# The last items of an attention stage and the start of the MLP: another order of masks, exponentials, one product and the low parts

## The chip, the cores and the metric

One core of a Trainium2 chip runs the whole program. TensorE (PE) does all products, VectorE (DVE), ScalarE (ACT) and GpSimd (POOL) the elementwise work, and SyncE (SP) issues every DMA. The metric is the device time of one execution in microseconds.

## What is computed

The input is 16 items of 128 tokens by 512 channels. Three stages follow each other: A is self attention with a mask, B is attention over a context, D is a gated attention at the end, and between B and D stands an MLP (512 to 2048 to 512). The part of the reference that matters here is the end of B and the MLP:

```
scores = jnp.einsum('bhqd,bhkd->bhqk', q, k) / jnp.sqrt(jnp.float32(HD))
scores = scores * mask - 10000.0 * (1.0 - mask)
probs = jax.nn.softmax(scores, axis=-1)
ctx = merge_heads(jnp.einsum('bhqk,bhkd->bhqd', probs, v))
x = x + ctx @ w_co + b_co
ln_out = layernorm(x, ln3_s, ln3_b)
mlp_out = gelu(ln_out @ w1 + b1) @ w2 + b2
```

There are 16 heads of 32 channels. Each fp32 operand of a large product is kept as a high part (rounded copy) and a low part (the rest), and a product is the sum of high by high, high by low and low by high.

## The kernel before

The program for each engine is written out by hand, engine by engine, and every wait is on a semaphore. An engine works strictly through its own list. Items are numbered g = 0 to 47 (16 to 31 are stage B). For an item PE makes `scores(g)`, DVE scales and masks them (`mask_scores`, two halves), POOL adds the mask bias (`add_mask_bias`, two halves), DVE takes the row maxima (`row_max`), ACT the exponentials in four quarters (`exps(g, 0..3)`), and DVE inverts the row sums (`inverse_sums`, L1825). PE then turns the inverted sums (`row_sums(g)`, L954) and the probabilities (`transpose_prob`, L933) through PSUM. ACT and DVE copy the turned probabilities back (`prob_out`, ACT quarters 0 and 2, DVE quarters 1 and 3), PE multiplies by the values (`times_v(g)`, L991), and after a split of the context into parts, `project_out(g)` (L1014). The turned row sums go out by ACT (`row_sums_out`, L1418) and over two DMAs of SP (`store_row_sums`, `spread_row_sums`) into the tile that `context(g)` reads.

The function `last_steps_of_b`, one per engine, handles items 30 and 31. In it PE has the MLP's first products between the attention's: `w1(p)` (L1075) makes 256 hidden channels of the first 256 tokens, and `w2(p)` (L1094) brings them back to 512. ACT adds the bias and squares (`hidden_out(p)`, L1496 and L1501), DVE makes the argument of the tanh (L1906), ACT the tanh (L1481), and DVE the high (`gelu_hi`, L1889 and L1897) and the low part (`gelu_lo`, L1901) that `w2(p)` waits for. `hidden_out(p)` also empties the PSUM bank: `project_out(28)` writes the bank of `w1(1)`, and `project_out(29)` that of `w1(3)`, so these two wait for the bias step of `hidden_out(1)` and `hidden_out(3)` (the semaphore `s_hx`).

Weights come in units of four chunks. `split((unit, c))` on ACT (L1337) makes a chunk's high part, on POOL (L2228) its low part. Units 12 and 14 are the third and fourth quarter of w1, 13 and 15 of w2. SP loads 13 and then 12 in step 13 of stage B, and 14 only after it has stored and spread the row sums of item 31:

```
store_row_sums(31)
spread_row_sums(31)
load_stream(31)
for c in range(KC):
    load_chunk((14, c))
```

`mlp_fill(1)` are the inputs for the second group of tokens, needed from `w1(8)` on: `turn_inputs` and `fill_hi` on DVE, `fill_scale` on ACT, `fill_lo` on POOL. PE's order from item 31 on is `times_v(29)`, `scores(31)`, `w1(2)`, `row_sums(30)`, transposes, `w1(3)`, transposes, `project_out(29)`, `times_v(30)`, `w1(4)`, `row_sums(31)`, transposes, `w2(0)`, `project_out(30)`, transposes, first half of `w2(1)`, `times_v(31)`, second half of `w2(1)`, `project_out(31)`, `w2(2)`, `w1(5)`, `w2(3)`, `w1(6)`, and on in this alternation.

Of the kernel before, what the change touches and what calls it, by code (L numbers as in the profile page):

```python
# [8 lines left out]
KC = H // 128  # L9
# [126 lines left out]
CHUNKS += [(u, c) for u in (12, 13, 14, 15, 16, 17, 18, 19) for c in range(KC)]  # L136
# [137 lines left out]
def build(nc, x, first_x, enc, encT, mask_a, mask_b, mask_d, weights, columns, rows, gate, ident_in, out):  # L274
# [3 lines left out]
    with ExitStack() as ctx:  # L278
# [566 lines left out]
        def pe_program():  # L845
# [232 lines left out]
            def w2(p, tiles=None):  # L1078
# [5 lines left out]
                if group.first == 0 and j % 2 == 0:  # L1084
                    pe.wait_ge(s_wlo, max(LO_COUNT[W2_UNIT[n], c] for c in range(KC)))
# [88 lines left out]
            def last_steps_of_b():  # L1174
# [18 lines left out]
                w1(4)  # L1193
                row_sums(31)
                transpose_prob(31, 0)
                transpose_prob(31, 1)
                w2(0)
# [133 lines left out]
        def act_program():  # L1331
# [230 lines left out]
            def last_steps_of_b():  # L1562
                for b in (14, 15):
                    g = 16 + b
                    if b == 14:
                        context_hi(g - 2, 0)
                        context_hi(g - 2, 1)
                    else:
                        tanh(0)
                    row_sums_out(g - 1)  # L1570
                    hidden_out(2 * b - 28)
                    prob_out(g - 1, 0)
                    for c in range(2 * b - 28, 2 * b - 26):
                        split((12, c))
                    hidden_out(2 * b - 27)
                    prob_out(g - 1, 2)
                    exps(g, 0)
                    exps(g, 1)
                    exps(g, 2)
                    if b == 14:  # L1580
                        context_hi(29, 0)
                        context_hi(29, 1)
                    exps(g, 3)
# [6 lines left out]
                for c in range(KC):  # L1590
                    split((13, c))
# [86 lines left out]
            for c in range(KC):  # L1678
                split((14, c))
            for p in range(5, NG * NPAIR):  # L1680
                g, jp = divmod(p, NPAIR)
                tanh(p - 1)
                hidden_out(p)
                if (g, jp) == (0, 5):
                    for c in range(KC):
                        split((15, c))
                    fill_scale(mlp_fill(1))
# [23 lines left out]
        def dve_program():  # L1711
# [300 lines left out]
            def last_steps_of_b():  # L2012
                for b in (14, 15):
                    g = 16 + b
                    context(g - 2, 0)
                    context(g - 2, 1)
                    if b == 14:
                        inverse_sums(g - 1)
                    context_lo(g - 2, 0)
                    context_lo(g - 2, 1)  # L2020
                    if b == 15:
# [412 lines left out]
```

## Time and profile before

| | us |
|---|---|
| median of 3 runs | 1086.4 |
| lowest and highest | 1083.62, 1086.55 |
| the profiled execution: its time | 1087.28 |
| the profiled execution: its span | 1085.7 |
| PE busy | 1066.5 (98%) |
| DVE, ACT, POOL busy | 820.6, 704.0, 483.4 |

The span is the time between the first and the last instruction of the profiled execution, and the time is 1.58 us more. The granted clock of TensorE is 1.00 in every stretch, its upper level. The last two items of B with the first MLP products stand between 466 and 545 us of the span.

### The profile page before, as it was taken

To read this page: it belongs to the slowest core of one execution; us is meant where nothing else is said; L and a number is where in the kernel's file an instruction comes from. 1 tells how busy PE (TensorE), PEld (TensorE's weight loads), DVE (VectorE), ACT (ScalarE), POOL (GpSimd) and SP (SyncE) were. 2 spreads that over 40 slices of the span, in tenths; PEclk is the share of its full clock that TensorE was granted. 3 is DMA by queue.
4 is the path that set the end of the run, shared out by engine and by line. 5 is a ranking of instruction groups with operands and counts; after the bars stand their busy time and mean duration, and the time that the engine had idled before them with its cause. 6 is when DMAs were issued, how large, how long until landed. Compare 5 with 4: busy or idle time off the path is not lost.

```text
span 1085.7 us, 24226 instructions
## 1 busy us (share of the span) xinstructions
PE 1066.5 (98%) x8741; PEld 924.1 (85%) x8741; DVE 820.6 (76%) x1303; ACT 704.0 (65%) x2355; POOL 483.4 (45%) x361
## 2 busy tenths in 40 slices
PE   8999999999999999999999999999999999999998
PEld 7889888888888888887898888888888998888886
DVE  8788777777888787888867667767697467777667
ACT  5787778677778787786444444444455276666676
POOL 4776555566777776767513122113032233333210
PEclk9999999999999999999999999999999999999999
DMA  7366666577777777564252151341647647777621
GB/s 248 104 190 209 202 206 192 187 190 223 221 217 216 222 216 227 180 193 139 85 155 98 59 174 59 117 141 53 214 136 257 229 127 207 223 209 210 195 61 60
DMA packets 145927, 185.92 MB, mean 171 GB/s; under 512 B 17952, under 2 KB 88848, under 8 KB 145808
## 3 DMA queue, kind: packets, MB, share of 16 engines
q1 hardware_dynamic: 145808, 184.37, 54.9%
q8 instruction: 70, 1.15, 0.5%
q14 instruction: 49, 0.40, 0.1%
HBM read 122.59 MB, written 61.73 MB: 170 GB/s over the span
## 4 chain that ended last, share of the span: by engine, by line
PE 66%; DVE 11%; DMA 7%; ACT 6%; POOL 4%; SPq 4%; issue 3%; DVEq 0%; ACTq 0%; POOLq 0%
PE psum L895 17%; PE psum L1094 15%; PE psum L1075 14%; PE psum L887 7%; PE psum L1014 6%; POOL prob L2267 3%; PE psum L913 2%; ACT prob L1409 2%; PE psum L991 2%; DMA ln_tile<-stream 2%; DMA normalised<-ln_tile 2%; DVE ln_tile L1739 2%; PE psum L933 2%; DVE negmax L1817 1%; SPq L558 1%
## 5 line engine op out<-in xcount | busy, mean ns | idle before, releaser
L895 PE MATMUL psum<-inputs_hi,weights_hi 128*128 128x256 f32 x768 | 224.2, 292 | 2.0 <-POOL inputs_lo L2253 1.4
L895 PE MATMUL psum<-inputs_lo,weights_hi 128*128 128x256 f32 x768 | 217.1, 283 | 0.0
L895 PE MATMUL psum<-inputs_hi,weights_lo 128*128 128x256 f32 x768 | 216.9, 282 | 0.0
L2267 POOL TENSOR_TENSOR prob<-prob,mask_bias 128x1024 f32<-128x1024 f32 x64 | 153.1, 2413 | 93.8 <-DVE prob L1804 93.2
L895 PEld LDWEIGHTS psum<-inputs_hi,weights_hi 128*128 128x128 f32 x768 | 146.6, 191 | 8.5 <-issue 2.9
L1817 DVE TENSOR_REDUCE negmax<-prob 128x8 f32<-128x1024 f32 x96 | 115.8, 1212 | 49.3 <-POOL prob L2267 49.1
L1409 ACT ACTIVATE prob<-prob,negmax 128x128 f32<-128x128 f32 x384 | 148.3, 391 | 0.5 <-DVE negmax L1817 0.5
L895 PEld LDWEIGHTS psum<-inputs_lo,weights_hi 128*128 128x128 f32 x768 | 147.0, 191 | 0.2
L895 PEld LDWEIGHTS psum<-inputs_hi,weights_lo 128*128 128x128 f32 x768 | 146.9, 191 | 0.0
L2253 POOL TENSOR_TENSOR inputs_lo<-inputs_transposed,inputs_hi 128x512 fp32r<-128x512 f32 x70 | 93.5, 1357 | 94.3 <-DVE inputs_hi L1777 60.5
L1409 ACT ACTIVATE prob_blocks<-prob,negmax 128x128 f32<-128x128 f32 x304 | 117.8, 391 | 19.4 <-DVE negmax L1817 19.3
L1014 PE MATMUL psum<-weights_hi,context_parts 128*128 128x512 f32 x376 | 125.8, 394 | 0.6 <-ACT qT L1355 0.3
L1496 ACT ACTIVATE qT<-psum,columns 128x512 f32<-128x512 f32 (+1 forms) x80 | 46.2, 598 | 96.9 <-PE psum L1075 96.9
L2270 POOL TENSOR_TENSOR residual<-residual,bias_rows 128x512 f32<-128x512 f32 x42 | 59.7, 1425 | 77.9 <-DMA residual<-stream 58.8
L1094 PE MATMUL psum<-weights_hi,hidden_parts 128*128 128x512 f32 x264 | 87.6, 392 | 1.1 <-DVE hidden_parts L1901 1.0
L1906 DVE SCALAR_TENSOR_TENSOR kT<-kT,qT 128x512 f32<-128x512 f32 x64 | 47.2, 737 | 51.9 <-ACT kT L1501 51.7
L1014 PEld LDWEIGHTS psum<-weights_hi,context_parts 128*128 128x128 f32 x376 | 70.7, 188 | 16.6 <-ACT qT L1496 0.6
L2228 POOL TENSOR_TENSOR weights_lo<-weights_whole,weights_hi 128x512 fp32r<-128x512 f32 x56 | 75.1, 1356 | 20.4 <-ACT weights_hi L1337 20.4
L1094 PE MATMUL psum<-weights_hi,context_parts 128*128 128x512 f32 x248 | 81.7, 390 | 0.9 <-DVE context_parts L1901 0.9
L1804 DVE SCALAR_TENSOR_TENSOR prob<-psum,mask 128x512 f32<-128x512 f32 x128 | 79.2, 680 | 2.9 <-ACT gate L1671 2.9
L1447 ACT ACTIVATE inputs_transposed<-inputs_transposed,columns 128x256 f32<-128x256 f32 x120 | 62.3, 590 | 27.6 <-DVE inputs_transposed L1746 27.6
L1075 PE MATMUL psum<-hidden_inputs,weights_hi 128*128 128x512 f32 x256 | 78.8, 389 | 0.0
(138 smaller groups left out, 2657.0 us busy)
## 6 DMA issues: line engine op xcount, KB each, us to landing
weights_whole<-weights_in SPq DMA_DIRECT2D x80, 256.0 KB, 3.8
prob_turned<-prob_blocks SPq DMA_DIRECT2D x38, 512.0 KB, 3.0
prob<-prob_turned SPq DMA_DIRECT2D x152, 128.0 KB, 3.5
inputs_transposed<-normalised SPq DMA_DIRECT2D x120, 128.0 KB, 2.8
normalised<-ln_tile SPq DMA_DIRECT2D x24, 512.0 KB, 2.8
context<-row_sums_spread SPq DMA_DIRECT2D x188, 64.0 KB, 2.1
stream<-residual SPq DMA_DIRECT2D x42, 256.0 KB, 2.9
ln_tile<-stream SPq DMA_DIRECT2D x32, 256.0 KB, 4.1
```

The source lines that it names most:

```text
L887: mm = pe.matmul(ps[:, bank, :], a[:, buf, c, tok], w[:, slot, c, :], start=c == 0 and i == 0, stop=c == KC - 1 and i == 2)
L895: mm = pe.matmul(ps[:, bank, GT * part:GT * part + GT], w[:, slot, c, o], a[:, buf, c, :], start=c == 0 and i == 0, stop=c == KC - 1 and i ...
L1014: mm = pe.matmul(ps[:, U_BANK + 1, :], a[0][:, cs], w[:, slot, c, :], start=c == 0 and i == 0, stop=c == KC - 1 and i == 2)
L1075: mm = pe.matmul(out, w[:, slot, c, o], a, start=c == 0 and i == 0, stop=c == KC - 1 and i == 2)
L1094: mm = pe.matmul(ps[:, accumulator(group, t), :], a[gb][:, tok], w[:, slot, (j * chunks + e) % 4, :], start=j == 0 and e == 0 and i == 0, ...
L1409: ins = act.activation(dst, src, ACT.Exp, bias=negmax[:, par, s:s + 1], accum_out=total[:, par, s:s + 1])
L1447: ins = act.activation(dst, src, ACT.Identity, bias=cols[:, b0 + c:b0 + c + 1], scale=cols[:, g0 + c:g0 + c + 1])
L1804: ins = dve.scalar_tensor_tensor(heads(P[:, 512 * c:512 * c + 512]), ps[:, S_BANK:S_BANK + 4, T * c:T * c + T], SCALE, other.unsqueeze(1). ...
L1817: dve.tensor_reduce(negmax[:, par, 8 * h:8 * h + 8], heads(prob[:, par, 1024 * h:1024 * h + 1024]), AX.X, ALU.max, negate=True).then_inc(s ...
L2228: pool.tensor_tensor(wlo[:, slot, c, :], raw[:, slot, c, :], whi[:, slot, c, :].bitcast(f32), ALU.subtract).then_inc(s_wlo, 1)
L2253: pool.tensor_tensor(lo, y, hi.bitcast(f32), ALU.subtract).then_inc(s_rlo if fill.ln is None else s_flo, 1)
L2267: pool.tensor_tensor(half, half, mb.unsqueeze(1).to_broadcast([128, 8, T]), ALU.add).then_inc(s_biased, 1)
```

## The change

It reorders work at the end of stage B and at the start of the MLP, on four engines; SP's list is untouched, and no engine has an operation more or less.

- DVE: the masking of items 30 and 31 goes ahead of the low parts of the context, and `inverse_sums` stands between or behind the halves. `prob_out` and `row_max` change places for item 31, and `prob_out(30, 3)` goes between `gelu_hi(0)` and `gelu_lo(0)`. `fill_hi(mlp_fill(1))` moves from step 5 to step 6, behind `gelu_lo(5)`.
- ACT: `exps(30, 0)` goes ahead of `hidden_out(1)`, `exps(31, 0)` ahead of `hidden_out(3)`, and `tanh(0)` behind `hidden_out(2)`. The splits of units 13 and 14 change places. `fill_scale(mlp_fill(1))` goes to step 6, ahead of `hidden_out(6)`, and the splits of unit 15 behind it.
- PE: `w2(0)` goes ahead of `row_sums(31)`, and `w2` of the first group waits chunk by chunk for the low parts of its weights.
- POOL: the splits of unit 14 wait for `s_glo` 3, that is for `gelu_lo(2)`; then come those of 13; `fill_lo(mlp_fill(1))` goes ahead of the splits of 15.

```diff
-CHUNKS += [(u, c) for u in (12, 13, 14, 15, 16, 17, 18, 19) for c in range(KC)]
+CHUNKS += [(u, c) for u in (12, 14, 13, 15, 16, 17, 18, 19) for c in range(KC)]
...
-                if group.first == 0 and j % 2 == 0:
-                    pe.wait_ge(s_wlo, max(LO_COUNT[W2_UNIT[n], c] for c in range(KC)))
+                if group.first == 0:
+                    pe.wait_ge(s_wlo, LO_COUNT[W2_UNIT[n], (j * chunks + chunks - 1) % 4])
...
                 w1(4)
+                w2(0)
                 row_sums(31)
                 transpose_prob(31, 0)
                 transpose_prob(31, 1)
-                w2(0)
...
+                context_hi(28, 0)
+                context_hi(28, 1)
+                row_sums_out(29)
+                hidden_out(0)
+                prob_out(29, 0)
+                split((12, 0))
+                split((12, 1))
+                exps(30, 0)
+                hidden_out(1)
+                prob_out(29, 2)
+                exps(30, 1)
+                exps(30, 2)
+                context_hi(29, 0)
+                context_hi(29, 1)
+                exps(30, 3)
+                row_sums_out(30)
+                hidden_out(2)
+                prob_out(30, 0)
+                tanh(0)
+                split((12, 2))
+                split((12, 3))
+                exps(31, 0)
+                hidden_out(3)
+                prob_out(30, 2)
+                exps(31, 1)
+                exps(31, 2)
+                exps(31, 3)
                 context_hi(30, 0)
                 context_hi(30, 1)
                 tanh(1)
...
                 prob_out(31, 0)
                 tanh(2)
                 for c in range(KC):
-                    split((13, c))
+                    split((14, c))
                 prob_out(31, 2)
                 hidden_out(4)
                 context_hi(31, 0)
...
             tanh(3)
             for c in range(KC):
-                split((14, c))
+                split((13, c))
             for p in range(5, NG * NPAIR):
                 g, jp = divmod(p, NPAIR)
                 tanh(p - 1)
+                if (g, jp) == (0, 6):
+                    fill_scale(mlp_fill(1))
                 hidden_out(p)
-                if (g, jp) == (0, 5):
+                if (g, jp) == (0, 6):
                     for c in range(KC):
                         split((15, c))
-                    fill_scale(mlp_fill(1))
...
+                context(28, 0)
+                context(28, 1)
+                make_mask_bias(30)
+                mask_scores(30, 0)
+                inverse_sums(29)
+                mask_scores(30, 1)
+                context_lo(28, 0)
+                context_lo(28, 1)
+                prob_out(29, 1)
+                row_max(30, 0)
+                row_max(30, 1)
+                prob_out(29, 3)
+                normalise(mlp_fill(1))
+                tanh_argument(0)
+                stream(28)
+                context(29, 0)
+                context(29, 1)
+                make_mask_bias(31)
+                mask_scores(31, 0)
+                mask_scores(31, 1)
+                inverse_sums(30)
+                context_lo(29, 0)
+                context_lo(29, 1)
+                row_max(31, 0)
+                prob_out(30, 1)
+                row_max(31, 1)
+                gelu_hi(0)
+                prob_out(30, 3)
+                gelu_lo(0)
+                tanh_argument(1)
+                stream(29)
...
+                    if g == 0:
+                        fill_hi(mlp_fill(1))
                     tanh_argument(p)
...
                 attention_residual(30)
+                attention_residual(31)
+                pool.wait_ge(s_glo, 3)
                 for c in range(KC):
-                    split((13, c))
-                attention_residual(31)
+                    split((14, c))
```

On ACT, at the start of step 30 before the change, from the last copy of item 29's quarter 0 on (`waits` are the semaphores; `w_hi` and `hidden` tell of weights and of `w1`):

```order
L1387 ACTIVATE prob<-psum 128x512 [waits prob_transposed]
L1337 ACTIVATE weights_hi<-weights_whole 128x512 [waits chunk0_loaded]
L1337 ACTIVATE weights_hi<-weights_whole 128x512 [waits chunk1_loaded]
L1496 ACTIVATE qT<-psum,columns 128x256 [waits hidden]
L1496 ACTIVATE qT<-psum,columns 128x256
L1501 ACTIVATE kT<-qT 128x512 [waits hidden_plus_bias]
L1387 ACTIVATE prob<-psum 128x512 [waits prob_transposed]
```

The same place after the change:

```order
L1387 ACTIVATE prob<-psum 128x512 [waits prob_transposed]
L1337 ACTIVATE weights_hi<-weights_whole 128x512 [waits chunk0_loaded]
L1337 ACTIVATE weights_hi<-weights_whole 128x512 [waits chunk1_loaded]
L1409 ACTIVATE prob,total<-prob,negmax 128x128 [waits row_sum_inverse,row_max]
L1409 ACTIVATE prob,total<-prob,negmax 128x128 x3
L1496 ACTIVATE qT<-psum,columns 128x256 [waits hidden]
L1496 ACTIVATE qT<-psum,columns 128x256
L1501 ACTIVATE kT<-qT 128x512 [waits hidden_plus_bias]
L1387 ACTIVATE prob<-psum 128x512 [waits prob_transposed]
```

Four exponentials now stand between the splits and the bias step of `hidden_out(1)`; item 31 has the same pattern with `hidden_out(3)`.

On PE, behind `w1(4)`, before the change (L954 is `row_sums(31)`, L1094 is `w2(0)`, whose first tile is shown):

```order
L1075 MATMUL psum<-inputs_hi,weights_lo 128x256
L954 MATMUL psum<-identity,rtotal 16x128 [waits stream_updated,row_sum_inverse]
L933 MATMUL psum<-identity,prob 128x128 [waits ctx_normalised,exps]
L933 MATMUL psum<-identity,prob 128x128 x3
L933 MATMUL psum<-identity,prob 128x128 [waits ctx_normalised,exps]
L933 MATMUL psum<-identity,prob 128x128 x3
L1094 MATMUL psum<-weights_hi,hidden_parts 128x512 [waits masked,w_lo,gelu_lo]
```

The same place after the change, with the whole of `w2(0)`:

```order
L1075 MATMUL psum<-inputs_hi,weights_lo 128x256
L1094 MATMUL psum<-weights_hi,hidden_parts 128x512 [waits masked,w_lo,gelu_lo]
L1094 MATMUL psum<-weights_lo,hidden_parts 128x512
L1094 MATMUL psum<-weights_hi,hidden_parts 128x512 x2
L1094 MATMUL psum<-weights_lo,hidden_parts 128x512
L1094 MATMUL psum<-weights_hi,hidden_parts 128x512
L1094 MATMUL psum<-weights_hi,hidden_parts 128x512 [waits masked]
L1094 MATMUL psum<-weights_lo,hidden_parts 128x512
L1094 MATMUL psum<-weights_hi,hidden_parts 128x512 x2
L1094 MATMUL psum<-weights_lo,hidden_parts 128x512
L1094 MATMUL psum<-weights_hi,hidden_parts 128x512
L954 MATMUL psum<-identity,rtotal 16x128 [waits stream_updated,row_sum_inverse]
```

The row sums of item 31, and all that follows from them on ACT and SP, now stand behind twelve products.

## Rows read from the trace of the kernel before

**Rows 1.** A stretch of the MLP: us, busy time of each engine (x instructions), clock, DMA

```profile
700.00:750.00 50.00, 50.00 (x222) 41.42 (x221) 36.28 (x55) 21.20 (x35) 15.18 (x12) 1.00 0.30 95
```

**Rows 2.** Timeline of PE: start us, length us, instruction [idle before it <-releaser]

```profile
476.00 0.50 PE L1014 MATMUL psum<-weights_hi,context_parts 128*128 128x512 f32 x1
...
481.07 0.39 PE L1075 MATMUL psum<-inputs_hi,weights_hi 128*128 128x256 f32 x1
...
485.16 0.28 PE L954 MATMUL psum<-identity,rtotal 128*16 128x128 f32 x1 [0.94 <-DVE rtotal L1825]
...
490.13 0.50 PE L1014 MATMUL psum<-weights_hi,context_parts 128*128 128x512 f32 x1
...
498.50 0.28 PE L954 MATMUL psum<-identity,rtotal 128*16 128x128 f32 x1 [1.19 <-DVE rtotal L1825]
...
499.42 0.47 PE L1094 MATMUL psum<-weights_hi,hidden_parts 128*128 128x512 f32 x1
...
502.27 0.39 PE L1014 MATMUL psum<-weights_hi,context_parts 128*128 128x512 f32 x1
...
507.33 1.08 PE L991 MATMUL psum<-prob,v 128*32 128x128 f32 x32
...
509.97 0.50 PE L1014 MATMUL psum<-weights_hi,context_parts 128*128 128x512 f32 x1
...
514.04 0.50 PE L1094 MATMUL psum<-weights_hi,hidden_parts 128*128 128x512 f32 x1 [1.03 <-DVE hidden_parts L1901]
...
532.13 0.50 PE L1094 MATMUL psum<-weights_hi,context_parts 128*128 128x512 f32 x1 [0.94 <-DVE context_parts L1901]
```

**Rows 3.** Timeline of ACT, end of B

```profile
475.11 0.84 ACT L1496 ACTIVATE qT<-psum,columns 128x256 f32<-128x256 f32 x2 [0.57 <-PE psum L1075]
...
483.18 0.39 ACT L1409 ACTIVATE prob<-prob,negmax 128x128 f32<-128x128 f32 x1
...
484.72 0.61 ACT L1481 ACTIVATE kT<-kT 128x512 f32<-128x512 f32 x1
...
489.24 0.84 ACT L1496 ACTIVATE qT<-psum,columns 128x256 f32<-128x256 f32 x2 [0.60 <-PE psum L1075]
...
499.16 0.25 ACT L1418 ACTIVATE row_sums_transposed<-psum 16x128 f32<-16x128 f32 x1
...
501.57 2.18 ACT L1337 ACTIVATE weights_hi<-weights_whole 128x512 fp32r<-128x512 f32 x4
505.63 0.60 ACT L1387 ACTIVATE prob<-psum 128x512 f32<-128x512 f32 x1 [1.89 <-PE psum L933]
```

**Rows 4.** Timeline of DVE, end of B and start of the MLP

```profile
469.51 0.26 DVE L1825 RECIPROCAL rtotal<-total 128x16 f32<-128x16 f32 x1 [1.07 <-ACT prob L1409]
...
470.63 2.48 DVE L1804 SCALAR_TENSOR_TENSOR prob<-psum,mask 128x512 f32<-128x512 f32 x4
...
474.44 1.22 DVE L1817 TENSOR_REDUCE negmax<-prob 128x8 f32<-128x1024 f32 x1 [0.73 <-POOL prob L2267]
...
510.89 1.41 DVE L1897 TENSOR_SCALAR hidden_parts<-kT 128x512 fp32r<-128x512 f32 x1
...
519.87 0.43 DVE L1897 TENSOR_SCALAR hidden_parts<-kT 128x512 fp32r<-128x512 f32 x1
...
526.13 2.10 DVE L1777 CAST inputs_hi<-inputs_transposed 128x512 fp32r<-128x512 f32 x2 [2.15 <-ACT inputs_transposed L1447]
```

**Rows 5.** Timeline of POOL: the two mask-bias halves of item 30

```profile
471.99 4.76 POOL L2267 TENSOR_TENSOR prob<-prob,mask_bias 128x1024 f32<-128x1024 f32 x2 [2.25 <-DVE prob L1804]
```

**Rows 6.** Timeline of SP's queue: the store of item 31's row sums

```profile
499.44 0.32 SPq L675 DMA_DIRECT2D row_sums_spread<-row_sums_transposed  x1
```

**Rows 7.** Tile weights_whole, 502.5 to 506 us: ns min/median/max, first and last start; landing

```profile
L617 SPq DMA_DIRECT2D weights_whole<-weights_in x4: 376/383/1105, 503.1 to 505.3; - x4
...
L2228 POOL TENSOR_TENSOR weights_lo<-weights_whole,weights_hi x3: 1292/1481/1738, 502.3 to 504.9; 128x512 fp32r<-128x512 f32 x3
...
DMA to landing us min/median/max: 3.6/3.8/4.2
```

More of the change, by code:

```diff
@@ L1562, in last_steps_of_b @@
             def last_steps_of_b():
[L1563 to L1583, printed above, removed]
+                context_hi(28, 0)
[25 more added lines that the diff above has]
+                exps(31, 3)
                 context_hi(30, 0)
@@ L2012, in last_steps_of_b @@
             def last_steps_of_b():
[L2013 to L2021, printed above, removed]
-                        inverse_sums(g - 1)
-                    make_mask_bias(g)
-                    mask_scores(g, 0)
-                    mask_scores(g, 1)
-                    prob_out(g - 1, 1)
-                    row_max(g, 0)
-                    row_max(g, 1)
-                    prob_out(g - 1, 3)
-                    if b == 14:
-                        normalise(mlp_fill(1))
-                    if b == 15:
-                        gelu_hi(0)
-                        gelu_lo(0)
-                    tanh_argument(b - 14)
-                    stream(g - 2)
+                context(28, 0)
[29 more added lines that the diff above has]
+                stream(29)
                 context(30, 0)
@@ L2193, in dve_program @@
                     turn_inputs(mlp_fill(1))
-                    fill_hi(mlp_fill(1))
                 if jp == (4 if g == 1 else 5) and 0 < g < NG - 1:
@@ L2350, in pool_program @@
             for c in range(KC):
-                split((14, c))
+                split((13, c))
             pool.wait_ge(s_row, 48)
@@ L2362, in pool_program @@
                     inverse_deviation(FILLS_OF_MLP[g][1])
-                if (g, jp) == (0, 5):
-                    for c in range(KC):
-                        split((15, c))
+                if (g, jp) == (0, 6):
                     fill_lo(mlp_fill(1))
+                    split((15, 0))
+                    split((15, 1))
                 if jp == 4 and ending:
@@ L2378, in pool_program @@
                     inverse_deviation(FILLS_OF_MLP[1][0])
+                    split((15, 2))
+                    split((15, 3))
             fill_lo(ln_fill(3, 1, 1))
```

## The prediction

> **What bounds the kernel now.** I read the busy shares first: TensorE is busy for 98% of the span, so nothing counts but what makes PE wait, or stop waiting. I then read the table of stretches: from 550 to 800 us PE has no idle time at all, as in [rows 1], where it is busy 50.00 of 50 us at the full clock. A delay or a gain that PE has at 540 us is therefore handed on unchanged to the end. So I went through the waits of PE and its timeline only between 466 and 545 us, where the change lies. PE idles there in four places [rows 2]: 0.94 us ahead of the row sums of item 30 and 1.19 us ahead of those of item 31 (both released by DVE's `inverse_sums`), 1.03 us ahead of `w2(2)` and 0.94 us ahead of `w2(5)` (both released by DVE's `gelu_lo`). They come to 4.1 us, which is the most that the change can take away, 0.38% of the time. Last I followed ACT, DVE, POOL and SP's queue through the same stretch, to see what each waiting instruction really hangs on.
>
> **Masks and exponentials of item 30.** Before, DVE idles 1.07 us for the last exponentials of item 29 (so from 468.44 on) and masks item 30 only from 470.63, in 2.48 us for both halves [rows 4]. The first half can now be done at about 468.44 + 0.2 + 1.24 = 469.9. POOL's bias takes 4.76 / 2 = 2.38 us a half [rows 5], so it ends at 472.3, and the row maximum of 1.22 us [rows 4], behind one copy, at about 474.1. ACT had been free since 475.11 - 0.57 = 474.54 and waited for `w1(1)` [rows 3]. It now starts `exps(30, 0)` there. A quarter takes 484.72 - 483.18 = 1.54 us [rows 3]. But `hidden_out(1)` stands behind it: it starts at 476.08 where it started at 475.11, its bias step ends 0.84 us later, and `project_out(28)`, which waits for that step to empty its bank, moves from 476.00 to 476.97. **A wait of 0.97 us is added here.** What PE would have found ahead of `row_sums(30)` is now used up: it ran out of work at 485.16 - 0.94 = 484.22 and now does so at 485.19. The inverse sums are there by then: scores(31) end when `w1(2)` starts, 481.07 before and about 482.1 now [rows 2], both masks take 2.48 us to 484.6, and the reciprocal 0.26 us to 484.85. So `row_sums(30)` stands at 485.2 as before at 485.16, and nothing is won by item 30.
>
> **Exponentials of item 31.** ACT was free at 489.24 - 0.60 = 488.64 ahead of `hidden_out(3)` [rows 3]. The tanh of the first product, now behind the row sums instead of ahead of them, moves this to about 489.1 (one instruction of 0.61 us, pipelined to 0.5). `exps(31, 0)` then ends at 490.6 and the bias step at 491.45. `project_out(29)` moves from 490.13 to about 491.5: **1.35 us are added**. From its start to the end of `w1(4)` PE has 498.50 - 1.19 - 490.13 = 7.18 us of work [rows 2], so it ends at 498.65. The 1.19 us wait would be gone by this alone.
>
> **`w2(0)` ahead of the row sums.** `w2(0)` takes 502.27 - 499.42 = 2.85 us [rows 2] and starts at about 498.5. So `row_sums(31)` goes from 498.50 to about 501.2, and `project_out(30)` stands at 502.1 where it stood at 502.27. Up to here PE has exchanged 0.94 + 1.19 us of one kind of wait for 0.97 + 1.35 us of another, and 0.15 us is won by the pipeline.
>
> **What hangs on these row sums.** This is the step that decides. ACT's `row_sums_out(31)` ended at 499.16 + 0.25 = 499.41; it began 0.66 us behind the transpose, when ACT had other work; now ACT waits for it, and I take 0.3, so that it ends at about 501.75. SP's store of the row sums followed at 499.44 [rows 6], then their spread, and the four loads of unit 14 from 503.1 on [rows 7]. All of this is in SP's fixed order and moves by 2.3 us. The last of the four was issued at 505.3, and they land 3.8 us after issue (3.6 to 4.2) [rows 7]: 509.1 before, 511.4 now. Before the change, ACT took unit 13 at this place, which had long been loaded: four splits from 501.57 in 2.18 us, and it then waited 1.89 us for the turned probabilities, so `prob_out(31, 2)` began at 505.63 [rows 3]. Now unit 14 stands there, ahead of `prob_out(31, 2)`. The last split ends at 511.4 + 0.6 = 512.0 and the copy of 0.60 us at 512.6. `times_v(31)` needs this copy, and behind it on PE stand half of `w2(1)` and `project_out(31)`; on ACT stand `hidden_out(4)` and `context_hi(31)`. **`times_v(31)` moves from 507.33 to 512.6, that is by 5.3 us.**
>
> From there to `project_out(31)` are 509.97 - 507.33 = 2.64 us, and twelve products take 2.85 us [rows 2]. `w2(2)` would so have come at 512.82 and came at 514.04. The wait ahead of it falls away: `gelu_lo(2)` ended 514.04 - 507.33 = 6.7 us behind the start of `times_v(31)`. Of this 1.0 us goes since POOL is held back (1.41 us of scaling at 510.89, 0.43 at 519.87 [rows 4]), and a tanh argument of 0.7 us is done during the wait. I take 5 us, so 517.6 (at worst 5.7, 0.2 us behind PE). `w2(2)` comes at 512.6 + 2.64 + 2.85 = 518.1: **4.1 us later than before**.
>
> **The fill and the low parts.** DVE waited 2.15 us for ACT's scaling ahead of `fill_hi(mlp_fill(1))` [rows 4], and `gelu_hi(5)` stood behind it; hence the wait ahead of `w2(5)`. Now `gelu_hi(5)` and `gelu_lo(5)` come first, and this wait goes: **1.1 us are won** (0.94 idle and 0.16 us in which the pipeline drains; both ends 0.9 and 1.2). POOL now waits for `gelu_lo(2)` at 517.6, and unit 14's four low parts take 1.29 to 1.74 us each [rows 7], median 1.48: done at 523.5. `w1(6)` wants them three products of 2.85 us behind `w2(2)`, at 526.6; unit 13's follow ahead of `w2(4)` and `w2(5)`, chunk by chunk. I cost this at nothing, and the cover is 3.1 us.
>
> **The sum.** 4.1 - 1.1 = +3.0 us; the roundings above lean late, so I take +2.9. On the profiled execution's 1087.28 us that is 1090.2; this one lies 0.9 us above the median of the runs, so against 1086.4 it is 1089.3. Bounds: one of SP's four issues took 1105 ns where the median is 383 [rows 7]; if that does not recur, 0.7 us less. Landing at 3.6 or 4.2 us moves it by -0.2 to +0.4. The two added waits can be off by 0.5 us together. The likeliest case's own range is 1087.8 to 1090.4.
>
> The four loads landed 3.8 us after issue [rows 7]. The Trainium skill, DMA: Bandwidth & Descriptors, Anatomy of one DMA, fits 2.0 us plus bytes over 436 GB/s for the path issued from GpSimd, which as an estimate gives 2.6 us for these 256 KB. By that page the last load would land 1.2 us sooner and the time would be 1088.1. The trace does not agree with it here, and the sum goes by the row.
>
> **The rivals.** First, **the loads do not hold ACT up**. Then `times_v(31)` comes at about 507.2, `w2(2)` at 512.7 (-1.3), and with the fill's 1.1 us the time is 1084.0. If the two waits for `hidden_out` don't arise either, up to 1.7 us more goes, to 1082.3. For it speaks that each step does shorten the chain it is aimed at, and that DVE scales in 0.43 us without POOL beside it and in 1.41 us with it [rows 4]. Against it speaks SP's order, which nothing changes: the last load would have to land before about 504.5, and 509.1 was its landing even with the earlier row sums. This decides the sign. Chance 14%, of which 8 points lie below 1083.1. The Trainium skill, SBUF — State Buffer, Who interferes with whom, says that GpSimd and such a VectorE instruction hold a common port in turn, for the whole instruction, and so backs the gain from holding the low parts back; the trace agrees with it in these two rows.
>
> Second, **the held-back low parts become a wait of their own**. If `gelu_lo(2)` comes later than 520.7 instead of 517.6, or POOL needs over 2.25 us a chunk, `w1(6)` waits, and on top of the 2.9 us come up to 2 more: 1091.3. The 3.1 us of cover speak against it, and the longest chunk of 1.74 us. Chance 12%, with any other added wait.
>
> Third, **the waits cancel**: with SP's short issue and quick landing the load wait costs 2 us less, and the result is 1087.3, no measurable change. Chance 14%. The forecast keeps 60%.
>
> **How the numbers follow.** A measurement of this kernel can tell about 0.3%, 3.3 us, from no change: above 1089.7 is slower, below 1083.1 faster. The forecast at 1089.3 lies just inside; its own range reaches 0.7 us beyond the bound, and 28 of its 60 points lie there. With the second rival's 12, slower has 0.40. Faster has 0.08, from the first rival. Within the bound are 32 + 6 + 14 points, 0.52. The range 1085.5 to 1091.2 leaves out most of the first rival and the worst of the second.
>
> **What the profile would show.** The first step is right if PE waits ahead of `project_out(28)` and `project_out(29)` for ACT's bias step, and L954 no longer waits. The deciding step is right if PE idles about 5 us ahead of `times_v(31)`, released by ACT, whose splits idle for a DMA. If ACT's splits run without idling, or PE's wait there is under 3 us, I am wrong. `w2(5)` should have no wait, and `w1(6)` none for POOL.

## The result, and the profile after

The changed kernel takes 1100.12 us (median of 4 runs, 1098.86 to 1102.46), beside 1086.47 us (4 runs, 1083.62 to 1086.87) for the kernel before on the same chip: a ratio of 1.0129 (95% interval 1.0115 to 1.0144). It is slower by 13.7 us where 2.9 us were forecast. The profiled execution has a span of 1099.4 us, 13.7 us more than before, and a mean granted clock of 0.994 instead of 1.00.

PE's timeline after the change, between 475 and 560 us (start, length, instruction, idle time before it and what ended it):

```profile
475.84 0.63 PE L933 MATMUL psum<-identity,prob 128*128 128x128 f32 x4 [0.64 <-DVE prob L1847]
479.27 0.80 PE L1014 MATMUL psum<-weights_hi,context_parts 128*128 128x512 f32 x1 [2.80 <-ACT qT L1496]
...
484.69 1.07 PE L991 MATMUL psum<-prob,v 128*32 128x128 f32 x24
...
507.03 0.27 PE L954 MATMUL psum<-identity,rtotal 128*16 128x128 f32 x1
...
507.93 0.48 PE L1014 MATMUL psum<-weights_hi,context_parts 128*128 128x512 f32 x1
...
519.42 1.94 PE L991 MATMUL psum<-prob,v 128*32 128x128 f32 x32 [6.25 <-ACT prob L1387]
...
523.43 0.39 PE L1014 MATMUL psum<-weights_hi,context_parts 128*128 128x512 f32 x1
...
526.16 0.39 PE L1094 MATMUL psum<-weights_hi,hidden_parts 128*128 128x512 f32 x1
...
538.37 0.50 PE L1094 MATMUL psum<-weights_hi,hidden_parts 128*128 128x512 f32 x1 [0.84 <-DVE hidden_parts L1908]
...
557.00 0.50 PE L1094 MATMUL psum<-weights_hi,context_parts 128*128 128x512 f32 x1 [1.34 <-DVE context_parts L1908]
```

Line numbers are 7 to 15 higher than before for DVE and POOL. Beside [rows 2]: the waits of 0.94 and 1.19 us ahead of L954, of 1.03 us ahead of `w2(2)` (526.16) and of 0.94 us ahead of `w2(5)` are gone, 4.1 us as forecast. In their place stand 0.64, 2.80, 1.18 (item 31's transposes, at 495.62), 1.08 (`project_out(29)`, at 497.33), 6.25, 0.84 and 1.34 us, 14.1 us together. That is +10.0 us. The rest is no wait. `project_out(28)` runs from 479.27 to 484.69, 5.42 us; the same twelve products took 478.96 - 476.00 = 2.96 us before. `times_v(31)` takes 521.29 - 519.42 = 1.87 us, where 1.02 us were enough in the second experiment below. The table of stretches shows why (busy time of PE, PE's loads, DVE, ACT and POOL, then the granted clock):

```profile
479.00:485.00 6.00, 5.73 (x20) 4.10 (x24) 1.26 (x3) 4.41 (x19) 0.00 (x0) 0.50 0.48 161
485.00:513.00 28.00, 25.73 (x244) 22.39 (x236) 21.08 (x32) 16.77 (x60) 10.04 (x6) 1.00 0.29 89
513.00:519.00 6.00, 0.17 (x1) 0.00 (x0) 0.72 (x2) 2.63 (x5) 1.26 (x1) 0.74 0.80 272
519.00:523.00 4.00, 3.58 (x37) 2.77 (x38) 1.84 (x5) 3.26 (x8) 0.00 (x0) 0.54 0.00 0
```

The granted clock is at its lower level, 1.2 GHz (0.50), behind the 2.80 us of idling, and falls again in the 6.25 us. The first costs 5.42 - 2.96 = 2.46 us, the second 1.87 - 1.02 = 0.85 us on `times_v(31)` and 2.14 - 1.62 = 0.52 us on the half of `w2(1)` behind it. Waits and clock come to 10.0 + 3.8 = 13.8 us.

**Why 2.80 us.** DVE between 469 and 478 us, after the change:

```profile
469.88 1.22 DVE L1811 SCALAR_TENSOR_TENSOR prob<-psum,mask 128x512 f32<-128x512 f32 x2
471.02 4.07 DVE L1859 TENSOR_TENSOR context_parts<-context,context_parts 128x256 fp32r<-128x256 f32 x2
475.02 0.68 DVE L1847 COPY prob<-psum 128x512 f32<-128x512 f32 x1
475.62 2.33 DVE L1824 TENSOR_REDUCE negmax<-prob 128x8 f32<-128x1024 f32 x2
```

POOL beside it:

```profile
469.87 4.94 POOL L2282 TENSOR_TENSOR prob<-prob,mask_bias 128x1024 f32<-128x1024 f32 x2 [0.39 <-DVE prob L1811]
```

and ACT's exponentials of item 30:

```profile
476.85 0.40 ACT L1409 ACTIVATE prob<-prob,negmax 128x128 f32<-128x128 f32 x1 [2.62 <-DVE negmax L1824]
...
478.41 0.81 ACT L1496 ACTIVATE qT<-psum,columns 128x256 f32<-128x256 f32 x2
```

The low parts of the context (L1859, two inputs in SBUF) now lie beside POOL's mask bias, which also reads SBUF. The pair takes 4.07 us; in the kernel before it stood at 469.81 us, ahead of POOL's start, and took 0.76 us. It ends when POOL's pair ends (475.0 and 474.8). So the first row maximum comes at 476.8 instead of the 474.1 that I worked out, and the four exponentials hold ACT's bias step, and PE, until 479.2.

**Why 6.25 us.** ACT between 514 and 520 us, after the change:

```profile
514.40 0.63 ACT L1337 ACTIVATE weights_hi<-weights_whole 128x512 fp32r<-128x512 f32 x1 [4.24 <-DMA weights_whole<-weights_in]
516.72 0.63 ACT L1337 ACTIVATE weights_hi<-weights_whole 128x512 fp32r<-128x512 f32 x1 [1.69 <-DMA weights_whole<-weights_in]
517.62 1.27 ACT L1337 ACTIVATE weights_hi<-weights_whole 128x512 fp32r<-128x512 f32 x2 [0.27 <-DMA weights_whole<-weights_in]
518.79 0.58 ACT L1387 ACTIVATE prob<-psum 128x512 f32<-128x512 f32 x1
```

and the tile's loads from 510 us on:

```profile
L617 SPq DMA_DIRECT2D weights_whole<-weights_in x4: 376/379/382, 511.5 to 512.9; - x4
...
DMA to landing us min/median/max: 2.9/5.0/5.4
```

ACT waits 6.2 us for unit 14 ahead of the copy that `times_v(31)` needs. The issues were short this time (382 ns at most), but the landings took up to 5.4 us, 4.2 at most in [rows 7].

### The profile page after: what moved, and what is told of

Its sections match the earlier page's. It is cut to its first block, busy times and chain, and to the rows that moved or that the text cites. A ratio compares the mean times of both kernels' runs of the same rounds, so it can differ in the third digit from the quotient of the medians.

```text
span 1099.4 us, 24232 instructions
## 1 busy us (share of the span) xinstructions
PE 1070.3 (97%) x8741; PEld 926.9 (84%) x8741; DVE 826.2 (75%) x1303; ACT 704.0 (64%) x2355; POOL 482.9 (44%) x361
## 4 chain that ended last, share of the span: by engine, by line
PE 68%; DVE 12%; ACT 6%; DMA 5%; issue 3%; SPq 3%; POOL 2%; DVEq 0%; ACTq 0%
PE psum L895 18%; PE psum L1094 14%; PE psum L1075 14%; PE psum L887 7%; PE psum L1014 7%; PE psum L913 3%; PE psum L991 3%; POOL prob L2282 2%; DMA ln_tile<-stream 2%; DMA normalised<-ln_tile 2%; ACT prob L1409 2%; PE psum L933 2%; DVE ln_tile L1746 2%; DVE negmax L1824 1%; DVE context_parts L1859 1%
## 5 line engine op out<-in xcount | busy, mean ns | idle before, releaser
L1094 PE MATMUL psum<-weights_hi,hidden_parts 128*128 128x512 f32 x264 | 88.0, 394 | 0.9 <-DVE hidden_parts L1908 0.8
L1094 PE MATMUL psum<-weights_hi,context_parts 128*128 128x512 f32 x248 | 81.6, 390 | 1.3 <-DVE context_parts L1908 1.3
```

The costliest lines, as they stand in the source:

```text
L1094: mm = pe.matmul(ps[:, accumulator(group, t), :], a[gb][:, tok], w[:, slot, (j * chunks + e) % 4, :], start=j == 0 and e == 0 and i == 0, ...
```

## The experiments

The kernel before measured 1086.46 us (9 runs) beside the first four kernels below, 1087.41 us (29 runs) beside the next four and 1086.33 us (24 runs) beside the last four; every ratio is to its own set. The whole change was not run again in them: what is said against it is a difference of medians to its 1100.12 us, and the kernel before's own medians differ by 1.1 us. The first theory had three causes: DVE's low parts beside POOL, ACT's order, and the clock. Four kernels each undo or cover one of them in the whole change.

**DVE's low parts behind the row maxima**, the whole change otherwise (item 31 alike):

```diff
-                context_lo(28, 0)
-                context_lo(28, 1)
                 prob_out(29, 1)
                 row_max(30, 0)
                 row_max(30, 1)
+                context_lo(28, 0)
+                context_lo(28, 1)
```

> The changed kernel with VectorE's low parts of the context of items 28 and 29 moved from ahead of the row maxima of items 30 and 31 to behind them. Theory P (these two-operand subtractions stand still while GpSimd adds the mask bias; 4.07 and 4.04 us for two instead of 0.76): the pair takes under 1 us again, the row maximum of item 30 is ready near 474.1 instead of 476.8, project_out(28) waits about 1 us instead of 2.80 and the clock does not fall there; item 31 likewise. Time 6 to 8 us below the changed kernel, near 1093. Rival Q (the pair is slow wherever it stands, and the exponentials ahead of hidden_out cost the wait): no more than 1 us below it.

Measured: 1095.45 us (4 runs), ratio 1.0079 (1.0053 to 1.0106), 4.7 us less than the whole change. The first line of `project_out(28)` in PE's timeline:

```profile
473.30 0.50 PE L1014 MATMUL psum<-weights_hi,context_parts 128*128 128x512 f32 x1 [0.91 <-ACT qT L1496]
```

It waits 0.91 us, where 0.97 was forecast, and `times_v(29)` follows at 476.25, 2.95 us later: full clock. So the 2.80 us were the forecast's wait plus DVE's pair beside POOL. The gain is smaller than the 6 to 8 us expected: the pair still takes 1.83 us where it stands now, and the wait ahead of `times_v(31)` is 7.14 us instead of 6.25, with a landing of up to 6.2 us.

**ACT's copy ahead of the splits of unit 14**, the whole change otherwise:

```diff
                 tanh(2)
+                prob_out(31, 2)
+                hidden_out(4)
+                context_hi(31, 0)
+                context_hi(31, 1)
                 for c in range(KC):
                     split((14, c))
-                prob_out(31, 2)
-                hidden_out(4)
-                context_hi(31, 0)
-                context_hi(31, 1)
```

> The changed kernel with ScalarE's prob_out(31, 2), hidden_out(4) and context_hi(31) ahead of the four splits of unit 14. Theory L (the splits wait for loads that stand in SyncE's list behind the row sums, and TensorE waits for the copy behind them): the wait of 6.25 us ahead of times_v(31) goes, and so does the half clock behind it; 7 to 8 us below the changed kernel, near 1092.5. Rival M (the wait only moves: the high parts of unit 14 come too late for w1(6)): a wait ahead of w1(6) of several us, and 3 us or less below it.

Measured: 1093.36 us (5 runs), ratio 1.0059 (1.0038 to 1.0079), 6.8 us less than the whole change. `times_v(31)` has no wait and full speed:

```profile
511.60 1.08 PE L991 MATMUL psum<-prob,v 128*32 128x128 f32 x32
```

**Exponentials behind the bias step**, the whole change otherwise (item 31 alike):

```diff
-                exps(30, 0)
                 hidden_out(1)
                 prob_out(29, 2)
+                exps(30, 0)
```

> The changed kernel with exps(30, 0) and exps(31, 0) back behind hidden_out(1) and hidden_out(3) and their copies. Theory E (what stands ahead of hidden_out holds project_out up): no wait ahead of project_out(28), whose products run at full clock; the row sums of items 30 and 31 wait 1 to 3 us again, since the maxima stay late behind the blocked low parts; 3 to 5 us below the changed kernel. Rival (the exponentials cost nothing there, the late maxima alone do): the wait comes back in full at the row sums, and the time is within 1 us of the changed kernel.

Measured: 1094.41 us (5 runs), ratio 1.0063 (1.0043 to 1.0083), 5.7 us less. The waits ahead of `project_out(28)` and `project_out(29)` are gone, and none stands ahead of the row sums, where 1 to 3 us were expected: these places on ACT won nothing. DVE's late pair costs 0.50 and 1.16 us ahead of the transposes all the same. The gain lies above the 3 to 5 us expected.

**PE kept busy in the two gaps**, the whole change otherwise. Transposes of the identity matrix into a free bank, whose results nobody reads, are added:

```diff
+                    if b == 14:
+                        pe.wait_ge(s_masked, 62)
+                        keep_busy(24)
                     pe.wait_ge(s_hx, 2 * b - 26)
                     project_out(g - 2)
...
                 w2(1, (0,))
+                keep_busy(54)
                 times_v(31)
...
+                for k in range(times):
+                    pe.transpose(ps[:, S_BANK, 128 * (k % 4):128 * (k % 4) + 128], ident[:, :], ident[:, :])
```

> The changed kernel with 24 transposes of the identity ahead of TensorE's wait for hidden_out(1) and 54 ahead of times_v(31), into a PSUM bank that nobody reads then, so that it does not stand idle. Theory C (TensorE's clock falls to its lower level after the idle stretches of 2.80 and 6.25 us and the next products run at half speed): granted clock 1.00 throughout, twelve products of project_out(28) in 2.9 us instead of 5.4, times_v(31) in 1.0 instead of 1.9; 3 to 4 us below the changed kernel. Rival (the slow products are late operands): no gain, or up to 0.5 us lost to the transposes.

Measured: 1096.22 us (4 runs), ratio 1.0087 (1.0067 to 1.0107), 3.9 us less with every dependence as in the whole change, and one more for the free bank. `project_out(28)` takes 2.94 us and `times_v(31)` 1.01 us. But the clock then fell behind the next gaps. In PE's timeline:

```profile
490.77 0.63 PE L933 MATMUL psum<-identity,prob 128*128 128x128 f32 x4 [1.18 <-DVE prob L1856]
492.49 0.50 PE L1014 MATMUL psum<-weights_hi,context_parts 128*128 128x512 f32 x1 [1.09 <-ACT qT L1505]
...
497.02 1.08 PE L991 MATMUL psum<-prob,v 128*32 128x128 f32 x32
```

`project_out(29)` takes 497.02 - 492.49 = 4.53 us. The clock is a cost of its own, beside the idling.

**All three edits together, and then without the hold-back.** The first kernel is the whole change with the edits of the first three experiments. The second also drops one line of POOL:

```diff
-                pool.wait_ge(s_glo, 3)
```

> The changed kernel with all three edits of the first experiments at once: low parts of the context behind the row maxima, exps(30, 0) and exps(31, 0) behind hidden_out(1) and (3), ScalarE's copy ahead of the splits of unit 14. If ports, order ahead of hidden_out and the late loads are the whole loss: no wait over 0.5 us before w2(2), clock 1.00, and the time lies 1 to 3 us below the kernel before. If GpSimd's held-back low parts cost something by themselves (waits of 0.8 to 1.4 us ahead of w2(4) and w2(7) seen after the change): these two waits stay, and it is within 2 us of the kernel before.

> The same without GpSimd's wait for gelu_lo(2). Theory H (held back, the eight low parts of units 14 and 13 run in one piece beside VectorE's GELU steps, and each scaling takes 1.4 instead of 0.43 us): the wait ahead of w2(4) goes, w2(7) may keep its wait, a wait near 1 us ahead of w2(2) can come back; 0 to 1.5 us below the one with the hold. Rival (the waits come from the fill's new place): both stay.

Measured: 1087.16 us (12 runs), ratio 1.0002 (0.9989 to 1.0014), and 1086.71 us (12 runs), ratio 0.9997 (0.9984 to 1.0010). The three edits take back all but 0.2 us: they hold the whole loss. What stays of the change has no worth to be measured, with the hold-back or without. Its waits are others than before, not fewer, and the expectation of none over 0.5 us ahead of `w2(2)` failed: with the hold-back PE waits 0.58 us ahead of `project_out(28)`, 0.71 us ahead of `row_sums(30)` and 1.17 us ahead of `times_v(30)`, where the view names no releaser ("issue"); DVE's copy `prob_out(30, 3)`, one that it needs, ends at 492.84 us.

```profile
492.94 1.08 PE L991 MATMUL psum<-prob,v 128*32 128x128 f32 x32 [1.17 <-issue]
```

PE's waits behind 500 us, with the hold-back:

```profile
523.72 0.50 PE L1094 MATMUL psum<-weights_hi,hidden_parts 128*128 128x512 f32 x1 [1.26 <-DVE hidden_parts L1908]
...
542.37 0.50 PE L1094 MATMUL psum<-weights_hi,context_parts 128*128 128x512 f32 x1 [1.39 <-DVE context_parts L1908]
```

and without it:

```profile
510.38 0.50 PE L1014 MATMUL psum<-weights_hi,context_parts 128*128 128x512 f32 x1 [0.50 <-DVE context_parts L1859]
...
515.53 0.50 PE L1094 MATMUL psum<-weights_hi,hidden_parts 128*128 128x512 f32 x1 [2.06 <-DVE hidden_parts L1908]
```

The hold-back mainly chooses which steps of DVE lie beside POOL's eight low parts. With it these run in one row of 12.22 us, and the steps for `w2(4)` and `w2(7)` are late; without it, those for `project_out(31)` and `w2(2)`.

**The swap of units 13 and 14 alone**, in the kernel before:

```diff
-CHUNKS += [(u, c) for u in (12, 13, 14, 15, 16, 17, 18, 19) for c in range(KC)]
+CHUNKS += [(u, c) for u in (12, 14, 13, 15, 16, 17, 18, 19) for c in range(KC)]
...
                 tanh(2)
                 for c in range(KC):
-                    split((13, c))
+                    split((14, c))
                 prob_out(31, 2)
...
```

The later splits of ACT and both groups of POOL change places in the same way.

> The kernel before with only units 13 and 14 exchanged (ScalarE splits 14 ahead of prob_out(31, 2)), nothing else moved. Theory L: with the row sums at their old time the last load lands near 509, the copy ends near 510.3, TensorE waits about 3 us ahead of times_v(31), and 1.8 to 3.5 us are lost, more if the clock falls. Rival (the wait came from the later row sums alone): under 1 us lost.

Measured: 1092.9 us (4 runs), ratio 1.0051 (1.0031 to 1.0071). ACT waits 5.19 and 0.49 us for the loads, and PE waits twice for the change, ahead of `times_v(31)` and of `w2(2)`:

```profile
499.20 0.28 PE L954 MATMUL psum<-identity,rtotal 128*16 128x128 f32 x1 [2.31 <-DVE rtotal L1825]
...
511.09 1.08 PE L991 MATMUL psum<-prob,v 128*32 128x128 f32 x32 [3.00 <-ACT prob L1387]
512.10 0.63 PE L1094 MATMUL psum<-weights_hi,hidden_parts 128*128 128x512 f32 x1
...
514.66 0.63 PE L1014 MATMUL psum<-weights_hi,context_parts 128*128 128x512 f32 x1
...
520.05 0.50 PE L1094 MATMUL psum<-weights_hi,hidden_parts 128*128 128x512 f32 x1 [1.97 <-DVE hidden_parts L1901]
```

This edit alone costs 5.5 us, without `w2(0)` ahead of the row sums. It is more than the 1.8 to 3.5 us expected for a full clock, and the clock fell here in a place of its own: behind the gap of 3.00 us `times_v(31)` still took its full-clock time (1.01 us), and only the products after it were slow, the half of `w2(1)` with 514.66 - 512.10 = 2.56 us instead of 1.62. The 2.31 us ahead of the row sums stand ahead of anything that this edit touches (see the last section).

**The masks alone**, in the kernel before:

```diff
-                    if b == 14:
-                        inverse_sums(g - 1)
-                    context_lo(g - 2, 0)
-                    context_lo(g - 2, 1)
-                    if b == 15:
-                        inverse_sums(g - 1)
                     make_mask_bias(g)
                     mask_scores(g, 0)
+                    inverse_sums(g - 1)
                     mask_scores(g, 1)
+                    context_lo(g - 2, 0)
+                    context_lo(g - 2, 1)
```

> The kernel before with only VectorE's masking of items 30 and 31 ahead of the low parts of the context. Theory P: the two low parts take 4 us beside GpSimd's mask bias instead of 0.76, the copies of the turned probabilities behind them make TensorE wait 0.5 and 1.2 us, and the row sums still wait; 0.5 to 3 us slower than before. Rival (earlier masks help where nothing else is moved): 1 to 2 us faster.

Measured: 1084.36 us (10 runs), ratio 0.9976 (0.9963 to 0.9989). **I was wrong here**: I expected a loss from DVE's pair, and it is a gain. The pair does take 4.08 us beside POOL, but ACT now has `hidden_out(1)` ahead of the exponentials and waits for nothing. Only the transposes wait for DVE, and the row sums' waits shrink by more:

```profile
475.02 0.63 PE L933 MATMUL psum<-identity,prob 128*128 128x128 f32 x4 [0.52 <-DVE prob L1840]
...
495.98 0.28 PE L954 MATMUL psum<-identity,rtotal 128*16 128x128 f32 x1 [0.53 <-DVE rtotal L1825]
```

The late pair is harmless by itself, and dear with the exponentials ahead of the bias step: the 2.80 us need both. (For item 31 the order is not quite that of the change: `inverse_sums` stands between the halves, and the pair takes 2.97 us.)

**The fill alone**, in the kernel before (ACT, DVE and POOL as in the change, PE untouched; ACT's part is shown):

```diff
                 tanh(p - 1)
+                if (g, jp) == (0, 6):
+                    fill_scale(mlp_fill(1))
                 hidden_out(p)
-                if (g, jp) == (0, 5):
+                if (g, jp) == (0, 6):
                     for c in range(KC):
                         split((15, c))
-                    fill_scale(mlp_fill(1))
```

> The kernel before with one part of the change alone: the second fill (scaling on ACT, high part on DVE behind gelu_lo(5), low part on POOL ahead of unit 15) moved to step 6. Theory (the fill's own wait was a true stall and nothing stands behind it): the 0.94 us ahead of w2(5) go and no new wait takes their place, so about 1.0 us less than the kernel before, 1085.4 us, ratio 0.999. Rival (the time is only handed on): the high part now stands between two steps of the MLP on DVE and w2(6) or w2(7) waits 0.5 to 1.4 us, as w2(7) does after the whole change (1.34 us); then 1086.5 us, or up to 0.4 us more.

Measured: 1086.37 us (11 runs), ratio 0.9991 (0.9980 to 1.0003). The wait of 0.94 us ahead of `w2(5)` is gone, and one of 0.21 us, for POOL, stands ahead of `w2(6)`:

```profile
536.43 0.47 PE L1094 MATMUL psum<-weights_hi,hidden_parts 128*128 128x512 f32 x1 [0.21 <-POOL weights_lo L2230]
```

Between these two 0.7 us are won in the trace, but a gain that small isn't told from none by the times.

**`w2(0)` ahead of the row sums alone**, in the kernel before:

```diff
                 w1(4)
+                w2(0)
                 row_sums(31)
                 transpose_prob(31, 0)
                 transpose_prob(31, 1)
-                w2(0)
```

> The kernel before with one part of the change alone: w2(0) ahead of row_sums(31); units 13 and 14 stay as they were. Theory (the harm came from the loads of unit 14 standing ahead of the copy, not from the late row sums): the row-sum wait of 1.19 us goes, ACT finds unit 13 long loaded, times_v(31) has no wait and comes about 1.2 us sooner; the wait ahead of w2(2) takes a part of that back (it was 1.03 us and may reach 2.2 us). 1085.3 to 1086.5 us. Rival (late row sums are the harm by themselves): the loads of unit 14 move 1.7 us and something behind times_v(31) waits, 2 us or more above the kernel before.

Measured: 1088.35 us (11 runs), ratio 1.0016 (1.0004 to 1.0028), 1.8 us above the upper end of the theory's range. The 1.19 us go, and PE is early, but `w2(2)` then waits for DVE's steps of `gelu_lo(2)`:

```profile
513.44 0.50 PE L1094 MATMUL psum<-weights_hi,hidden_parts 128*128 128x512 f32 x1 [3.13 <-DVE hidden_parts L1901]
...
517.89 0.28 PE L1075 MATMUL psum<-inputs_hi,weights_hi 128*128 128x256 f32 x1
```

The wait grew from 1.03 to 3.13 us, more than the 1.19 us that had gone, and `w2(2)` then takes 517.89 - 513.44 = 4.45 us instead of 2.85, since the clock has fallen. Waits from the row sums of item 31 on are 4.08 us where they were 3.16, and the clock adds 1.6. (The start of `w2(2)` at 513.44 looks 0.6 us early, but this execution was 1.8 us early already at `row_sums(30)`, ahead of the edit.) PE arrives sooner, and the `gelu_lo(2)` that it waits for comes later: two of DVE's steps ahead of it now lie beside POOL's work and take 2.04 and 1.77 us, 0.95 and 0.68 before:

```profile
506.57 2.04 DVE L1852 TENSOR_TENSOR context_parts<-context,context_parts 128x256 fp32r<-128x256 f32 x2 [0.16 <-ACT context_parts L1433]
508.54 1.77 DVE L1889 SCALAR_TENSOR_TENSOR kT<-kT,qT 128x512 f32<-128x512 f32 x1
```

Neither theory had this. Nothing waited for the late row sums or for the loads behind them ahead of `times_v(31)`; the harm came at `w2(2)`.

**SP's loads of unit 14 ahead of the row-sum store**, the whole change otherwise:

```diff
+            for c in range(KC):
+                load_chunk((14, c))
             store_row_sums(31)
             spread_row_sums(31)
             load_stream(31)
-            for c in range(KC):
-                load_chunk((14, c))
```

> The whole change, with SP's four loads of unit 14 ahead of the store of item 31's row sums instead of behind. ACT's order is left as changed. Theory (ACT's copy for times_v(31) hung on the landing of these loads, as the prediction's fourth step says): they are issued from about 501.5 us on and have landed by 507.5 us, ACT's splits wait for nothing, the wait of 6.25 us ahead of times_v(31) goes to under 0.7 us and the half clock behind it too; about 7 us less than the whole change, 1093.2 us, the same as with the copy moved ahead of the splits. Rival (the two added places on ACT, not the DMA, held it up): a wait of 2 us or more stays, and with it the clock's fall: 1096 us or more.

Measured: 1092.48 us (4 runs), ratio 1.0057 (1.0043 to 1.0071), 7.6 us less than the whole change. ACT's order is untouched, and it waits for no load:

```profile
508.16 2.18 ACT L1337 ACTIVATE weights_hi<-weights_whole 128x512 fp32r<-128x512 f32 x4
510.25 0.58 ACT L1387 ACTIVATE prob<-psum 128x512 f32<-128x512 f32 x1
```

It was the landing of the loads, and nothing in ACT's own work. The clock is not mended by this: it fell behind the 2.81 us ahead of `project_out(28)` (4.29 us instead of 2.96), behind 1.19 and 1.09 us ahead of `project_out(29)` (4.43 us instead of 2.96) and behind 1.77 us ahead of `w2(4)`.

```profile
493.96 0.80 PE L1014 MATMUL psum<-weights_hi,context_parts 128*128 128x512 f32 x1 [1.09 <-ACT qT L1496]
```

**Masks and fill together**, in the kernel before, the edits as shown:

> The kernel before with the two parts that looked harmless: DVE's masks of items 30 and 31 ahead of the low parts of the context (measured alone at 1084.4 us) and the second fill moved to step 6. Theory (the two remove different waits and share no cover): the gains add up, about 2.1 + 1.0 us below the kernel before, 1083.4 us, ratio 0.997. Rival (the wait ahead of w2(2) or one ahead of w2(7) takes the fill's gain): 1084.4 us, as with the masks alone.

Measured: 1084.05 us (8 runs), ratio 0.9972 (0.9961 to 0.9983). This version beats both kernels. From the masks alone (1084.36) it differs by less than can be told, so whether the gains add up stays open.

## Why the prediction was wrong

The sign and the mechanism of the largest term were right, the size was off by 10.8 us. Step by step:

- **Masks and exponentials of item 30: the step that failed first.** It put the row maximum at 474.1 us, "behind one copy", and so the added wait at 0.97 us. Between mask and copy stands the pair of low parts, which I costed as if POOL beside it did not matter. Measured 2.80 us, plus 0.64 us ahead of the transposes: 2.5 us too little. With the pair out of the way the wait was 0.91 us, so the rest of the step was right. The prediction cited the Trainium skill, SBUF — State Buffer, Who interferes with whom, for a gain from holding POOL back; the same section says that a VectorE instruction with two SBUF inputs contends with a GpSimd one that reads SBUF. That applies to this pair, and I did not look for places where the change itself makes such a meeting. The trace agrees with it: 4.07 us against 0.76.
- **The clock: no term at all.** I asked for each wait how long it was and never whether PE's clock would outlast it. Measured 2.46 and 1.37 us; filling the gaps gave 3.9 us back.
- **Exponentials of item 31.** Forecast 1.35 us, measured 1.08, plus 1.18 us ahead of the transposes, from DVE's second pair beside POOL (4.04 us).
- **`w2(0)` ahead.** The two row-sum waits went, as forecast. Alone, the move is a small loss (1088.35 us), since `w2(2)` then waits longer.
- **What hangs on the row sums.** The mechanism was right (ACT's splits stand for the DMA, PE behind them), shown from both sides: by the copy moved ahead and by the loads moved ahead. The size: `times_v(31)` moved 507.33 to 519.42, that is 12.1 us, of which 5.7 are from before `project_out(30)`. The step itself is 6.4 us where I had 5.3: a landing of up to 5.4 us instead of 3.8, less 0.5 us or so for four short issues (511.5 to 512.9 us, 503.1 to 505.3 before).
- **`w2(2)` and the fill.** Both waits went, as forecast.
- **The hold-back, costed at nothing.** I looked at whether POOL's low parts would come in time for PE, and they did. I did not look at what POOL's eight in a row do to DVE beside them: 0.84 and 1.34 us ahead of `w2(4)` and `w2(7)`, 2.2 us together. That the second comes from there too is argued: with the fill alone DVE's steps for `w2(6)` and `w2(7)` are as long, and `w2(7)` has no wait, so DVE must have been late when it came to them.

The missed amounts are 2.5 + 3.8 + 0.9 (item 31) + 1.1 + 2.2 = 10.5 us of 10.8. The three single mendings give back 4.7, 6.8 and 5.7 us, 17.2 in sum, and together 13.0 (13.5 with each kernel held against the kernel before of its own set). They overlap: the first and the third both remove the 2.80 us gap or the most of it, and its fall of the clock.

## What to carry to other kernels

When a two-input step of VectorE is moved, look at what GpSimd does at its new place. Here one moved by 1.2 us became five times as long. On an in-order engine, put nothing that waits for a late load ahead of a copy that PE needs; the order of the loads is to be changed first. And price a wait of PE by its length and by the products behind it: in these traces a gap of 2.8 to 3.1 us cost 1.3 to 2.5 us more than itself. Short waits close together are not safe either: 1.18 and 1.09 us ahead of `project_out(29)` cost 1.6 us in the kernel with the fillers, while 1.18 and 1.08 us cost nothing in the whole change.

## What was not expected of the hardware

The kernel before loses a little clock too, in some executions. In the three sets together its 62 executions have a mean granted clock of 1.000 (38 of them, mean 1086.3 us) or 0.998 (24, mean 1088.2 us): 1.9 us apart. With the masks alone all 10 were at 1.000, and with masks and fill all 8; with `w2(0)` ahead alone 9 of 11 were at 0.998 or 0.997. The profile of the kernel before is one of those at 1.00, so where the clock falls in the others isn't seen. But a part of what the masks bring is probably this: 1084.8 us on average lie 1.8 us below the 1086.6 us of the kernel before's executions at full clock in the same set, and 2.5 us below the mean of all.

Gaps of like size did not all end alike. After 2.16 us (the fill alone, ahead of the row sums) the clock stayed at 1.00. After 2.06 us (no hold-back, ahead of `w2(2)`, with 0.50 us shortly before) `w2(2)` took 4.4 us. After 3.00 us (the swap alone) it held for all of `times_v(31)` and fell behind it; after 2.80 us (the whole change) the first product was slow. What decides between these, beside the length of the wait, stays open.

The wait of 1.19 us ahead of item 31's row sums is not the same in every execution either. With the fill alone it is 2.16 us and with the swap alone 2.31 us, and up to there both have the lists of the kernel before. In these two traces a step of DVE lies beside POOL's addition to the residual and takes 1.67 and 1.78 us; in the kernel before's trace the same two steps take 0.69 us each. The 4.1 us of waits that the prediction set out from are those of one execution.
